# A router front of 28 hand-ordered steps: the transposes move one step behind the normalisation, logits and gates one step further

## The chip, the cores and the metric

The kernel runs on one core of a Trainium2 chip. The metric is the device time of one execution in microseconds (us). The core has a matrix engine (TensorE, PE in the rows), a vector engine (VectorE, DVE), a scalar engine (ScalarE, ACT), GpSimd (POOL) and SyncE (SP), which here only issues DMAs. Each engine works through its own list of instructions in order, and they wait for one another by semaphores.

## The reference

The program is one transformer-like stack over 16 sequences of 512 tokens of 256 features: attention, a mixture of experts, a forget attention, and the same mixture of experts again, each on a layer norm of its input and added to it. The part that matters is the mixture:

```
x      = layernorm(hidden)                      # 8192 x 256
logits = x @ router_w.T                         # 64 experts
probs  = softmax(logits); top 8 kept, rescaled to sum 1
routed = the 8 chosen experts' gated products (at most 128 slots a block), weighted
gu     = x @ ws_gate_up                         # shared expert
shared = (silu(gu[:, :192]) * gu[:, 192:]) @ ws_down
out    = hidden + routed + shared
```

## The kernel before

The program runs as blocks, one after another: `attention_project`, `attention_mix`, then `moe_front` and `moe_experts` for the first mixture (tiles named m1f and m1e), `forget_attention`, and `moe_front` and `moe_experts` again (m2f and m2e). The change is in `moe_front`, which therefore runs twice.

`moe_front` takes the 8192 tokens in 16 rounds of 512 (4 tiles of 128 tokens). For a round s it does this:

- SP loads x (`load`, L936, 512 KB) into a ring of 3.
- DVE takes mean and variance (`statistics` L1040, `aggregate` L1047) and POOL makes 1/deviation and shift (`inverse_deviation`, L997 to L1008).
- ACT normalises x into `row[:, s % 4]` (`normalise`, L1130, four instructions). `row` is a ring of RB = 4 buffers of 640 KB: 256 normalised features and 64 gates for each token.
- PE transposes the round in two halves (`turn_x(0)`, `turn_x(1)`, L1184) through one PSUM tile, `ps_x`, and ACT copies each half out (`keep(0)`, `keep(1)`, L1136). The second half waits until the first is copied out.
- PE computes the logits (L1193). DVE finds the eight largest (L1052), marks them, subtracts the largest, makes `chosen`; ACT takes the exponential (L1142); DVE picks and sums (`pick`, L1071 to L1075); POOL scales (`gates`, L1013), which fills the last part of the round's `row`.
- SP stores the finished `row` (`store_rows`, L944). Only when it has landed may `normalise` of round s + 4 write that buffer.
- PE counts tokens for each expert (`count_tiles`, L1200).
- The shared expert: `gate_up(0..2)` (L1212, twelve matmuls), silu on ACT (L1147, L1149), products on DVE (L1081, L1086), `down_first` and `down_rest` on PE (L1219, L1226), copies on ACT (`copy_down`, L1159), the residual (L940) added on POOL (L1020), and the store (L948).

All of it is ordered by hand. Each engine calls `in_turn(stages)` with a list of (at, stage, items). For s = 0 to STEPS - 1 = 27 it goes through the list and issues each stage whose `at(i)` is s. So an engine's order is: by step, and within the step by its list. There is no barrier between steps; an engine goes on as soon as its own waits allow.

Before the change round i is loaded and measured in step i, normalised and transposed in step i + 1, given logits in step i + 2, and gated, stored and counted in step i + 3. The shared expert's gate and up products of round r run in step 2r + 2 for r < 8 and in r + 10 after that, and the down product one step later. So up to step 17 two kinds of step alternate. In this text a G step has the gate and up products and a D step the down product. In steps 19 to 26 the places of the tokens are worked out for two groups of 4 experts a step (`climb` L1244 and L1245, `copy_rise` L1164 on ACT, `find_place` L1255, `count_below` L1103 on DVE), next to the last shared products. `count_reached` (L1262) ends it in step 27.

PE's list begins: `logits`, `turn_x(0)`, even `climb`, `gate_up(0)`, `down_first`, `turn_x(1)`, ... , `down_rest`, `gate_up(1)`, ..., `gate_up(2)`, `count_tiles`. ACT's list is `normalise`, `keep(0)`, `keep(1)`, `copy_rise`, `copy_down`, `exponential`, `silu`. SP's list is `load`, weight loads, `load_residual`, `store_rows`, `store`. The lines that the change's consequences hang on are these:

```
def normalise(s):
    act.wait_ge(shift_done, s + 1)
    wait(act, row_stored[s % RB], 16 * (s // RB))
...
def turn_x(q):
        pe.wait_ge(xn_done, TPR * s + 2 * q + 2)
        wait(pe, x_kept, 2 * s + q)
```

Of the kernel before, what the change touches and what calls it, by code (L numbers as in the profile page):

```python
# [10 lines left out]
def wait(eng, sem, value):  # L11

    if not isinstance(value, int) or value > 0:
        eng.wait_ge(sem, value)  # L14
# [784 lines left out]
def moe_front(nc, tag, dram, x_in, x_out, const):  # L799
# [8 lines left out]
    ROUNDS, S = TILES // TPR, TPR * P  # L808
# [5 lines left out]
    GROUPS = E // GROUP  # L814
    slots, slots_f = const["slots"], const["slots_f"]

    L_NORM, L_LOGITS, L_GATE = 1, 2, 3
    EARLY = ROUNDS // 2
    COUNTED = ROUNDS + L_GATE
    ASSIGN = [COUNTED + k // 2 for k in range(GROUPS)]  # L820

    def shared_at(r):
        return 2 * r + 2 if r < EARLY else r + EARLY + 2

    STEPS = shared_at(ROUNDS - 1) + 3

    with ExitStack() as ctx:
# [82 lines left out]
        def x_of(s):  # L910

            return const["ahead_x"][:].rearrange("p (t d) -> p t d", d=D) if ahead and s == 0 else x[:, s % XB]

        def kept_at(r):

            return (r - 6) % XT
# [4 lines left out]
        def in_turn(stages):  # L921

            for s in range(STEPS):
                for at, stage, items in stages:
                    for i in range(items):
                        if at(i) == s:
                            stage(i)

        @block.sync
        def _(sp):  # L930
# [41 lines left out]
            def load_kept(i):  # L972
                sp.wait_ge(gated, 3 * (last_round(i) + 1))
                load_weights(OWN + EARLY_BUFFERS + i)

            in_turn([(lambda i: i, lambda i: load(i + XB - 1), ROUNDS - XB + 1), (lambda i: ROUNDS + i, load_weights, OWN),
                     (lambda i: ROUNDS + L_GATE + 1 + i, load_early, EARLY_BUFFERS), (lambda i: shared_at(last_round(i)) + 1, load_kept, KEPT_BUFFERS),
                     (shared_at, load_residual, ROUNDS),
                     (lambda i: i + L_GATE, store_rows, ROUNDS), (lambda r: shared_at(r) + 1, store, ROUNDS)])
            sp.wait_ge(pad_stored, 16)  # L980
# [142 lines left out]
        @block.scalar  # L1123
        def _(act):
# [3 lines that stand above are left out]
                wait(act, x_was_turned, 2 * (s - RB + 1))  # L1128
                for t in range(TPR):
                    nc.scalar.activation(row[:, s % RB, t, 0:D], x_of(s)[:, t, :], ACT.Identity, bias=shift_x[:, s % 2, t], scale=rstd[:, s % 2, t]).then_inc(xn_done, 1)  # L1130

            def keep(q):
                def stage(s):
                    act.wait_ge(x_was_turned, 2 * s + q + 1)
                    wait(act, gated, 3 * (s - XT + 1))
                    nc.scalar.activation(x_turned[:, kept_at(s), :, 2 * q * P:2 * (q + 1) * P], ps_x[:], ACT.Copy).then_inc(x_kept, 1)  # L1136
                return stage

            def exponential(s):
                act.wait_ge(logit_done, s + 1)  # L1140
                wait(act, picked_done, s - 1)
                nc.scalar.activation(expd[:, s % 2], logit[:, s % 2], ACT.Exp).then_inc(exp_done, 1)  # L1142

            def silu(r):
                wait(act, h_done, 2 * (r - 1))
                act.wait_ge(gated, 3 * r + 1)
                nc.scalar.activation(act_g[:, r % 2, 0, :], ps_h[0][:], ACT.Silu).then_inc(silu_done, 1)  # L1147
                act.wait_ge(gated, 3 * r + 3)
                nc.scalar.activation(act_g[0:SR, r % 2, 1, :], ps_h[2][0:SR, :], ACT.Silu).then_inc(silu_done, 1)  # L1149

            def copy_down(r):
                wait(act, stored[r % 2], 16 * (r // 2))
                if r == 0 and ahead:

                    for landed, value in const["x_stored"]:
                        act.wait_ge(landed, value)
                act.wait_ge(down_done, r + 1)
                for q in range(2):
                    nc.scalar.activation(xo[:, r % 2, 2 * q:2 * q + 2, :], ps_d[q][:], ACT.Copy).then_inc(down_copied, 1)  # L1159

            def copy_rise(k):
                act.wait_ge(rise_ready, k + 1)
                wait(act, place_ready, k - 1)
                nc.scalar.activation(rise[:, k % 2], ps_x[0:E].rearrange("p c t -> p (c t)"), ACT.Copy).then_inc(rise_done, 1)  # L1164

            in_turn([(lambda i: i + L_NORM, normalise, ROUNDS), (lambda i: i + L_NORM, keep(0), ROUNDS), (lambda i: i + L_NORM, keep(1), ROUNDS), (lambda k: ASSIGN[k], copy_rise, GROUPS),
                     (lambda r: shared_at(r) + 1, copy_down, ROUNDS), (lambda i: i + L_LOGITS, exponential, ROUNDS), (shared_at, silu, ROUNDS)])

        @block.tensor
        def _(pe):  # L1170
# [7 lines left out]
            def turn_x(q):  # L1178
                def stage(s):
                    pe.wait_ge(xn_done, TPR * s + 2 * q + 2)  # L1180
                    wait(pe, x_kept, 2 * s + q)
                    for t in range(2):
                        for c in range(2):
                            last = nc.tensor.transpose(ps_x[:, c, t * P:(t + 1) * P], row[:, s % RB, 2 * q + t, c * P:(c + 1) * P], ident[:])  # L1184
                    last.then_inc(x_was_turned, 1)
                return stage
# [17 lines left out]
            def gate_up(i):  # L1204
                def stage(r):
                    if i == 0:
                        pe.wait_ge(x_kept, 2 * (r + 1))
                        wait(pe, silu_done, 2 * (r - 1) + 1)
                    else:
                        wait(pe, h_done, 2 * (r - 1) + i)  # L1210
                    for c in range(2):
                        last = nc.tensor.matmul(ps_h[i][:], w_gu[:, c, i, :], x_turned[:, kept_at(r), c, :], start=c == 0, stop=c == 1)  # L1212
                    last.then_inc(gated, 1)
                return stage
# [43 lines left out]
            def count_reached(k):  # L1258
                pe.wait_ge(rise_done, GROUPS)
                pe.wait_ge(reached_done, GROUPS)  # L1260
                for e in range(E):
# [3 lines left out]
            even = lambda k: ASSIGN[k] if k % 2 == 0 else -1  # L1265
            odd = lambda k: ASSIGN[k] if k % 2 else -1
            down_at = lambda r: shared_at(r) + 1
            in_turn([(lambda i: i + L_LOGITS, logits, ROUNDS), (lambda i: i + L_NORM, turn_x(0), ROUNDS), (even, climb, GROUPS),
                     (shared_at, gate_up(0), ROUNDS), (down_at, down_first, ROUNDS), (lambda i: i + L_NORM, turn_x(1), ROUNDS), (even, find_place, GROUPS),
                     (odd, climb, GROUPS), (down_at, down_rest, ROUNDS), (shared_at, gate_up(1), ROUNDS), (odd, find_place, GROUPS),  # L1270
                     (shared_at, gate_up(2), ROUNDS), (lambda i: i + L_GATE, count_tiles, ROUNDS), (lambda i: STEPS - 1, count_reached, 1)])

# [752 lines left out]
def program(nc, a):  # L2025
# [18 lines left out]
    def mixture(tag, x_in, x_out, x_stored):  # L2044
        with (nc.sbuf_tensor(tag + "_slots", [P, E], u32) as slots, nc.sbuf_tensor(tag + "_slots_f", [P, E], fp32) as slots_f,
              nc.sbuf_tensor(tag + "_own", [P, OWN * (GU + WD) - WD], fp32) as own, nc.sbuf_tensor(tag + "_early", [P, EARLY * (GU + WD)], fp32) as early,
              nc.sbuf_tensor(tag + "_kept", [P, KEPT * (GU + WD)], fp32) as kept):


            buffers = []  # L2050
            for memory, n in ((own, OWN), (early, EARLY), (kept, KEPT)):
                for k in range(n):
                    at = k * (GU + WD) - (WD if memory is own and k > 0 else 0)
                    down = ahead_x[0:F // 2, :] if memory is own and k == 0 else memory[0:F // 2, at + GU:at + GU + WD]
                    buffers.append((memory[:, at:at + GU].rearrange("p (j m c f) -> p j m c f", j=2, m=2, c=2),
                                    down.rearrange("p (j c d) -> p j c d", j=2, c=2)))
            const = dict(held, **landing, x_stored=x_stored, slots=slots, slots_f=slots_f, w_buffers=buffers, early=early, kept=kept, w_gate=a["L0_ffn_w_gate"], w_up=a["L0_ffn_w_up"], w_down=a["L0_ffn_w_down"])
            with nc.cleanup_on_exit():
                moe_front(nc, tag, routed, x_in, x_out, const)
            with nc.cleanup_on_exit():  # L2060
                moe_experts(nc, tag, routed, x_out, const)
# [69 lines left out]
```

## Time and profile before

| what | us |
|---|---|
| median of 3 runs (lowest, highest) | 2587.7 (2587.27, 2588.34) |
| the profiled execution, its time | 2572.92 |
| its span in the trace | 2571.3 |
| first front, from its first instruction to its last store | 1108.2 to 1348 |
| second front | 2090.4 to 2338 |
| granted TensorE clock, mean over the span | 0.961 |

The profiled execution is 14.8 us shorter than the median of the runs. In the rows, a time is in us from the start of the span; a line of the timeline gives start, duration, engine, source line, operation, tiles, the number of instructions merged, and in brackets how long the engine sat idle before it and what ended that. The granted clock is 1.00 at 2.4 GHz and 0.50 at 1.2 GHz.

### The profile page before, as it was taken

Reading aid. Unit: us, or ns where it says so; the run is one execution under the profiler, and the core shown is the slowest. Engines: PE = TensorE matmul, PEld = TensorE weight load, DVE = VectorE, ACT = ScalarE, POOL = GpSimd, SP = SyncE. Lnnn points to the kernel's source line nnn. Section 1 sums busy time; section 2 is a strip of 40 time slices with the busy share of each in tenths; the row PEclk is TensorE's granted clock in tenths of the full one; section 3 lists DMA queues with packets and bytes.
Section 4 is the critical chain, followed back from the end, with each engine's and each line's share of the span. In section 5 each row is a group of like instructions: output and inputs, shape, how many; then the busy total and the mean of one; then the engine's idle time right before and its main releaser. Section 6 shows DMA issues by size and latency. Waiting matters only on the chain. (4 is left out here: it accounts for less than half of the span.)

```text
span 2571.3 us, 47983 instructions
## 1 busy us (share of the span) xinstructions
PE 2413.5 (94%) x14630; PEld 1324.0 (51%) x14630; DVE 1650.9 (64%) x3745; ACT 1374.3 (53%) x2766; POOL 1151.7 (45%) x1497
## 2 busy tenths in 40 slices
PE   7997999999999999979999996999999969998998
PEld 4664233333333333356556774566666645655775
DVE  6777888888888888446553333788888746553332
ACT  4666677667766776646532333455555436632332
POOL 6998111110111011123226775777777723325776
PEclk9998799999999999989999998999999988898999
DMA  5655423232333332136777984011111025595996
GB/s 176 204 193 174 124 85 99 87 98 87 95 90 91 93 91 68 35 118 205 224 236 202 231 200 71 18 38 38 35 38 34 20 75 182 189 291 162 223 230 108
DMA packets 290964, 325.17 MB, mean 126 GB/s; under 512 B 30496, under 2 KB 272368, under 8 KB 290800
## 3 DMA queue, kind: packets, MB, share of 16 engines
q1 hardware_dynamic: 257024, 274.22, 35.3%
q0 software_dynamic: 29184, 46.43, 8.8%
q10 hardware_dynamic: 4592, 2.47, 0.4%
q8 instruction: 87, 1.43, 0.2%
q14 instruction: 77, 0.63, 0.1%
HBM read 217.29 MB, written 105.19 MB: 125 GB/s over the span
## 5 line engine op out<-in xcount | busy, mean ns | idle before, releaser
L716 DVE TENSOR_REDUCE a_row_max<-a_ps_m 128x2 f32<-128x1024 f32 x512 | 607.6, 1220 | 84.1 <-PE a_ps_m L619 79.3
L776 ACT ACTIVATE a_probs<-a_ps_s 128x512 f32<-128x512 f32 x1024 | 536.8, 601 | 206.4 <-PE a_ps_s L647 206.1
L662 PE MATMUL a_ps_o<-a_probs,a_va 128*32 128x512 f32 x2048 | 273.8, 607 | 0.8 <-ACT a_o_sb L785 0.8
L1731 POOL TENSOR_TENSOR b_spread<-b_decay,held_own_sb 128x512 f32<-128x512 f32 x256 | 269.2, 1084 | 8.2 <-DVE b_weight L1792 8.2
L1792 DVE TENSOR_TENSOR b_weight<-b_ps_s,b_spread 128x512 f32<-128x512 f32 x256 | 163.8, 683 | 17.6 <-PE b_ps_s L1932 17.6
L647 PE MATMUL a_ps_s<-first_qs,first_ks 98*128 98x512 bf16 (+1 forms) x512 | 160.8, 395 | 3.2 <-DMA first_qs<-a_m_parts 3.2
L647 PE MATMUL a_ps_s<-second 98*128 98x512 bf16 (+1 forms) x512 | 156.8, 386 | 4.8 <-DMA second<-a_m_parts 2.3
L556 POOL CAST a_high<-a_row_max 128x32 bf16<-128x32 f32 x32 | 6.6, 206 | 316.6 <-DVE a_row_max L716 316.6
L597 POOL DMA_DIRECT2D x<-a_xo x32 | 24.2, 757 | 274.0 <-DVE a_xo L750 271.6
L315 PE MATMUL a_ps_qk<-a_w_qk,a_xnT 128*128 128x512 f32 x256 | 121.7, 598 | 0.0
L619 PE MATMUL a_ps_m<-first_ks,first_qs 48*128 48x512 bf16 x512 | 106.4, 413 | 10.0 <-DVE a_row_max L716 9.3
L619 PEld LDWEIGHTS a_ps_m<-first_ks,first_qs 48*128 48x128 bf16 x512 | 24.7, 93 | 158.2 <-issue 90.5
L1212 PE MATMUL m2f_ps_h<-m_kept,held_ws_gate_up_sb 128*128 128x512 f32 x192 | 103.8, 677 | 0.0
L1868 ACT ACTIVATE b_o_sb<-b_ps_o,held_b_den_eps 128x512 f32<-128x512 f32 x64 | 44.0, 688 | 111.4 <-PE b_ps_o L1942 111.4
L619 PEld LDWEIGHTS a_ps_m<-second 48*128 48x128 bf16 x512 | 24.5, 92 | 147.7 <-issue 94.8
L1551 DVE SCALAR_TENSOR_TENSOR m1e_h<-m1e_act_g,m1e_xg,m1e_ps_h 128x192 f32<-128x192 f32 x64 | 26.5, 414 | 115.3 <-ACT m1e_act_g L1480 115.3
L1551 DVE SCALAR_TENSOR_TENSOR m2e_h<-m2e_act_g,m2e_xg,m2e_ps_h 128x192 f32<-128x192 f32 x64 | 26.5, 414 | 115.1 <-ACT m2e_act_g L1480 115.1
L619 PE MATMUL a_ps_m<-second 48*128 48x512 bf16 x512 | 99.8, 386 | 0.4
L1212 PE MATMUL m1f_ps_h<-m_kept,held_ws_gate_up_sb 128*128 128x512 f32 x192 | 100.0, 655 | 0.0
L198 POOL TENSOR_TENSOR a_qk<-a_rot_cos,a_rot_sin 128x512 f32<-128x512 f32 x64 | 81.4, 1272 | 7.5 <-DVE a_rot_sin L240 7.5
L647 PEld LDWEIGHTS a_ps_s<-second 98*128 98x128 bf16 (+1 forms) x512 | 37.8, 97 | 84.7 <-issue 39.6
L191 POOL TENSOR_TENSOR second<-a_rest,second 128x512 bf16<-128x512 f32 x64 | 74.2, 1160 | 10.9 <-ACT second L286 5.4
(397 smaller groups left out, 5454.2 us busy)
## 6 DMA issues: line engine op xcount, KB each, us to landing
parts<-second SPq DMA_DIRECT2D x16, 1536.0 KB, 6.2
second<-parts SPq DMA_DIRECT2D x384, 64.0 KB, 2.3
rows<-m_early SPq DMA_DIRECT2D x32, 640.0 KB, 3.2
m_early<-x SPq DMA_DIRECT2D x31, 512.0 KB, 4.0
first_qs<-parts SPq DMA_DIRECT2D x192, 64.0 KB, 2.3
first_ks<-parts SPq DMA_DIRECT2D x192, 64.0 KB, 2.2
m_own<-in_L_ffn_w_gate_dram SPq DMA_DIRECT2D x24, 384.0 KB, 4.3
m_own<-in_L_ffn_w_up_dram SPq DMA_DIRECT2D x24, 384.0 KB, 5.6
```

Source lines behind the costliest of these rows:

```text
L191: nc.gpsimd.tensor_tensor(parts[:, k // TPB, 2, :, j * P:(j + 1) * P], rest[:, u, :].rearrange("p (g t) -> p g t", g=4), parts[:, k // TPB ...
L198: nc.gpsimd.tensor_tensor(qk[:, u, :], rot_cos[:, u, :], rot_sin[:, u, :], ALU.add).then_inc(qk_done, 1)
L315: last = nc.tensor.matmul(ps_qk[u][:], xnT[:, u, c, :], w_qk[:, c, :], start=c == 0, stop=c == 1)
L619: last = nc.tensor.matmul(m_bank(name, step)[:, e, :], qs[u][rows, 2 * n.p + e, t * P:(t + 1) * P], ks[u][rows, 2 * n.p + e, :], start=Tru ...
L647: nc.tensor.matmul(s_bank(name, step)[:], ks[u][0:K_ALL[e], h, t * P:(t + 1) * P], qs[u][0:K_ALL[e], h, :], start=True, stop=True).then_in ...
L662: last = nc.tensor.matmul(ps_o[VW * j:VW * (j + 1), :], va[n.u][:, t, (h0 + j) * VW:(h0 + j + 1) * VW], probs[:, group % 2, j, t, :], star ...
L716: nc.vector.tensor_reduce(row_max[:, n.k // 4 % 2, t, :, n.p % 4], m_bank(name, step)[:], AX.X, ALU.max).then_inc(m_drained, 1)
L776: nc.scalar.activation(probs[:, group % 2, j, t, :], s_bank(name, step)[:], ACT.Exp, scale=DK ** -0.5).then_inc(s_drained, 1)
L1212: last = nc.tensor.matmul(ps_h[i][:], w_gu[:, c, i, :], x_turned[:, kept_at(r), c, :], start=c == 0, stop=c == 1)
L1551: nc.vector.scalar_tensor_tensor(h[:, i % 2, j, :], act_g[:, i % 2, j, :], xg[:, i % XB, j, D + e:D + e + 1], ps_h[j][:, 1, :], ALU.mult, ...
L1731: nc.gpsimd.tensor_tensor(spread[:, n % 2, heads].rearrange("p h t c -> p (h t) c"), decay[:, n % 3, heads].rearrange("p h (t o) -> p (h t ...
L1792: nc.vector.tensor_tensor(weight[:, n % 2, heads, :], ps_s[r][:].rearrange("p h (j t) -> p (h j) t", t=P), spread[:, n % 2, heads].rearran ...
```

## The change

Round i is still measured in step i and normalised in step i + 1. It is transposed in step i + 2 (new constant L_TURN), given logits in step i + 3, and gated, stored and counted in step i + 4. The shared products of rounds 0 to 7 move from step 2r + 2 to 2r + 3; those of rounds 8 to 15 stay in r + 10. COUNTED and with it the steps of the places become 20 to 27 instead of 19 to 26. The number of steps (28), the order within each list, and all ring sizes stay. No instruction is added or removed.

```diff
-    L_NORM, L_LOGITS, L_GATE = 1, 2, 3
+    L_NORM, L_TURN, L_LOGITS, L_GATE = 1, 2, 3, 4
     EARLY = ROUNDS // 2
     COUNTED = ROUNDS + L_GATE
     ASSIGN = [COUNTED + k // 2 for k in range(GROUPS)]
 
     def shared_at(r):
-        return 2 * r + 2 if r < EARLY else r + EARLY + 2
+        return 2 * r + 3 if r < EARLY else r + EARLY + 2
...
-            in_turn([(lambda i: i + L_NORM, normalise, ROUNDS), (lambda i: i + L_NORM, keep(0), ROUNDS), (lambda i: i + L_NORM, keep(1), ROUNDS), (lambda k: ASSIGN[k], copy_rise, GROUPS),
+            in_turn([(lambda i: i + L_NORM, normalise, ROUNDS), (lambda i: i + L_TURN, keep(0), ROUNDS), (lambda i: i + L_TURN, keep(1), ROUNDS), (lambda k: ASSIGN[k], copy_rise, GROUPS),
...
-            in_turn([(lambda i: i + L_LOGITS, logits, ROUNDS), (lambda i: i + L_NORM, turn_x(0), ROUNDS), (even, climb, GROUPS),
-                     (shared_at, gate_up(0), ROUNDS), (down_at, down_first, ROUNDS), (lambda i: i + L_NORM, turn_x(1), ROUNDS), (even, find_place, GROUPS),
+            in_turn([(lambda i: i + L_LOGITS, logits, ROUNDS), (lambda i: i + L_TURN, turn_x(0), ROUNDS), (even, climb, GROUPS),
+                     (shared_at, gate_up(0), ROUNDS), (down_at, down_first, ROUNDS), (lambda i: i + L_TURN, turn_x(1), ROUNDS), (even, find_place, GROUPS),
```

## Rows read from the trace of the kernel before

**Rows 1.** The page: busy time of each engine and share of the span.
```profile
PE 2413.5 (94%) x14630; PEld 1324.0 (51%) x14630; DVE 1650.9 (64%) x3745; ACT 1374.3 (53%) x2766; POOL 1151.7 (45%) x1497
```

**Rows 2.** Waits of TensorE, first front, steps 4 to 16: total, times, longest.
```profile
PE m1f_ps_x L1184 <- ACT m_early L1130: 10.2, 7, 1.5
```

**Rows 3.** Stretches: length; busy PE, PEld, DVE, ACT, POOL; granted clock, DMA share, GB/s.
```profile
1139.70:1246.40 106.70, 97.98 (x504) 64.86 (x504) 67.53 (x319) 71.07 (x122) 41.19 (x73) 0.92 0.56 182
2123.60:2236.40 112.80, 104.03 (x504) 67.78 (x504) 67.65 (x320) 71.33 (x122) 41.30 (x73) 0.86 0.54 173
1208.90:1214.20 5.30, 5.30 (x13) 3.13 (x14) 3.65 (x13) 1.48 (x3) 3.17 (x6) 0.50 0.84 270
```

**Rows 4.** Timeline of TensorE: a D step, a G step, next logits; the last pair.
```profile
1148.21 2.00 PE L1193 MATMUL m1f_ps_l<-m1f_rwT,m_kept 128*128 128x64 f32 x16
...
1152.51 0.66 PE L1184 MATMUL m1f_ps_x<-held_ident_sb,m_early 128*128 128x128 f32 x4
...
1154.51 2.00 PE L1193 MATMUL m1f_ps_l<-m1f_rwT,m_kept 128*128 128x64 f32 x16
1157.92 0.66 PE L1184 MATMUL m1f_ps_x<-held_ident_sb,m_early 128*128 128x128 f32 x4 [1.41 <-ACT m_early L1130]
1160.13 0.60 PE L1184 MATMUL m1f_ps_x<-held_ident_sb,m_early 128*128 128x128 f32 x4
1160.57 3.60 PE L1212 MATMUL m1f_ps_h<-m_kept,held_ws_gate_up_sb 128*128 128x512 f32 x8
...
1164.65 2.00 PE L1193 MATMUL m1f_ps_l<-m1f_rwT,m_kept 128*128 128x64 f32 x16
...
1246.51 1.12 PE L1184 MATMUL m1f_ps_x<-held_ident_sb,m_early 128*128 128x128 f32 x4 [1.47 <-ACT m_early L1130]
...
1256.16 2.00 PE L1193 MATMUL m1f_ps_l<-m1f_rwT,m_kept 128*128 128x64 f32 x16
```

**Rows 5.** Timeline of ScalarE, the same D and G steps.
```profile
1154.07 1.09 ACT L1159 ACTIVATE m1f_xo<-m1f_ps_d 128x512 f32<-128x512 f32 x2 [0.27 <-PE m1f_ps_d L1219]
1155.17 1.28 ACT L1142 ACT_TABLE_LOAD   x1
1156.46 0.42 ACT L1142 ACTIVATE m_early<-m_early 128x256 f32<-128x256 f32 x1
1156.79 2.06 ACT L1130 ACTIVATE m_early<-m_early,m1f_shift_x,m1f_rstd 128x256 f32<-128x256 f32 x4
1158.76 0.58 ACT L1136 ACTIVATE m_kept<-m1f_ps_x 128x512 f32<-128x512 f32 x1
...
1164.69 2.06 ACT L1130 ACTIVATE m_early<-m_early,m1f_shift_x,m1f_rstd 128x256 f32<-128x256 f32 x4
```

**Rows 6.** Timeline of SyncE's DMA issues, the same G step.
```profile
1156.53 0.37 SPq L944 DMA_DIRECT2D rows<-m_early  x1
1159.39 0.51 SPq L936 DMA_DIRECT2D m_early<-x  x1
1159.94 1.05 SPq L940 DMA_DIRECT2D m1f_xr<-x  x1
1163.34 0.37 SPq L944 DMA_DIRECT2D rows<-m_early  x1
```

**Rows 7.** The row stores (L944) by themselves: in that D step, then all of them.
```profile
DMA to landing us min/median/max: 3.2/3.2/3.2
...
DMA to landing us min/median/max: 3.2/3.2/8.4
```

**Rows 8.** Timeline, filling of the first front.
```profile
1115.56 0.20 POOL L1008 TENSOR_TENSOR m1f_shift_x<-m1f_minus_mean,m1f_rstd 128x4 f32<-128x4 f32 x1
...
1116.47 1.09 PE L1184 MATMUL m1f_ps_x<-held_ident_sb,m_early 128*128 128x128 f32 x4 [0.78 <-ACT m_kept L1136]
```

**Rows 9.** Timeline of TensorE and ScalarE, the last step with places.
```profile
1342.58 0.38 PE L1255 MATMUL m1f_ps_l<-m1f_rise,m1f_reached 64*128 64x128 bf16 x4
...
1343.57 0.59 ACT L1164 ACTIVATE m1f_rise<-m1f_ps_x 64x512 bf16<-64x512 f32 x1 [3.40 <-PE m1f_ps_x L1245]
```

## The prediction

> **What bounds the kernel now.** I read the page first, then the waits of TensorE, then busy times by stretch, and last the timeline of three engines over one pair of steps. TensorE is busy 94% of the span [rows 1] and the blocks follow one another, so a front that is longer by 1 us makes the program longer by 1 us. A measurement tells a change from none from about 0.2% on (5.2 us). Inside the first front TensorE waits seven times for the normalisation, 10.2 us in all [rows 2]; the second front shows the same seven. Each stands where a G step follows a D step. The timeline shows why: ScalarE has copy_down, a table load and the exponential to do (1154.07 to 1156.88) before it starts `normalise` at 1156.79 [rows 5], and the transposition wants its first two tiles, so it starts at 1157.92 after 1.41 us of idle [rows 4].
>
> The clock costs as much again. A pair of steps takes 1164.65 - 1148.21 = 16.44 us where the clock stays at 2.4 GHz [rows 4]. Six pairs of the first front take 106.7 us and six of the second 112.8 us [rows 3], 17.78 and 18.80 us a pair, so 1.34 and 2.36 us a pair, 1.85 on average, go to a lower clock. After one of those waits the granted clock is 0.50, that is 1.2 GHz, for 5.3 us [rows 3]. The last G step takes 1256.16 - 1246.51 = 9.65 us from its first transpose instead of 1164.65 - 1157.92 = 6.73 us [rows 4], 2.92 us more.
>
> **What moves.** No instruction is added, so busy time at full clock is unchanged. TensorE's order up to the last transposition is the old one, one step number later. Relative to it, only ScalarE's `normalise`, the statistics on VectorE and GpSimd and SyncE's `load` run one step earlier. So I lay the new steps over the times of the pair in rows 4 to 6.
>
> *What is removed.* `turn_x(0)` uses rows normalised a step ago. It starts 1.41 us earlier, and left alone `turn_x(1)` would start at 1160.13 - 1.41 = 1158.7.
>
> *What is late next.* `normalise(s)` writes `row[s % 4]` and waits for the store of round s - 4 to land. Before, that store was issued in step s - 1, and `normalise(s)` is in step s + 1: a whole step of slack. Now `gates`, and `store_rows` behind it, are one step later, so the store is issued in step s, just ahead of the normalisation that waits for it. In the D step the store is issued at 1156.53 [rows 6] and takes 3.2 us to land [rows 7]. It hangs on the logits of the D step through VectorE and GpSimd, none of which moves against TensorE. It lands at 1159.73. `normalise`, ready at 1156.79 as before [rows 5], is held 2.95 us.
>
> Queued behind it on ScalarE is `keep(0)`, and `turn_x(1)` needs that copy. So: landing 1159.75, four normalisations of 2.06 us to 1161.8, the copy 0.6 us to 1162.4, some 0.14 us to TensorE (an estimate: half of the normalisations of 1156.79 are over at 1157.8, and the transposition that wants them starts at 1157.92 [rows 4, 5]), `turn_x(1)` at 1162.55. It was at 1160.13 [rows 4]: **+2.4 us a pair**. TensorE idles from about 1158.8, some 3.8 us in one piece instead of 1.4.
>
> The landing may differ. The store is alone in the queues at this point of the pair, as it was before, so 3.2 us is the value; the largest landing of a row store is 8.4 us [rows 7], for stores behind weight loads, which do not exist in these steps.
>
> The Trainium skill (DMA: Bandwidth & Descriptors, section Anatomy of one DMA) gives a DMA about 2.0 us of fixed cost and then its bytes at 436 GB/s. For 640 KB that is an estimate of 3.5 us where this trace has 3.2, which would add 0.3 us to each of twelve waits and give 2624.5. Its fixed part also says that a smaller store would still be held up, which no run here shows.
>
> *How often.* `normalise(4)` is the first with an earlier user of its buffer. It and rounds 6, 8, 10, 12 and 14 fall where a G step follows a D step: six a front, twelve in all.
>
> *The clock in these twelve pairs.* It was 1.85 us a pair. The new gap is longer, and the row nearest to a sure drop is the last pair, 2.92. I take 2.2, between them. The bounds are 0 (as in the pair of rows 4, which waited and lost nothing) and everything behind the gap at half speed, `turn_x(1)` and eight matmuls, 0.5 + 3.6 us [rows 4], so +4.1. Each pair then changes by 2.4 + 2.2 - 1.85 = 2.75 us, **12 x 2.75 = +33.0**; with the bounds 2.4 + 0 - 1.85 = 0.55 and 2.4 + 4.1 - 1.85 = 4.65.
>
> *The last pair of each front.* There is no round 16, so nothing is held and `turn_x(0)` doesn't wait: 1.47 and 2.92 us are saved [rows 4]. **2 x -4.4 = -8.8.**
>
> *Filling.* `normalise(1)` now comes ahead of `keep(0)` of round 0. Its shift is ready at 1115.76 [rows 8]; 2.06 and 0.6 us later, with 0.14, `turn_x(1)` of round 0 starts at 1118.55, not 1116.47 [rows 8]. **2 x 2.1 = +4.2.** The first waits of `normalise(0)` are the same.
>
> *Step 18.* It now has the logits of round 15, and `silu` of round 8 stands behind copy_down, the exponential and two table loads: 1.09 + 1.28 + 0.42 + 1.28 + 0.6 = 4.7 us [rows 5] (the last two are the same kinds of instruction), 5.0 with its start. TensorE has four to five microseconds of products behind `down_rest` to cover it. I take 0.5; bounds 0 and 1. **+1.0.**
>
> *The tail.* Steps 19 to 25 of before hide two groups' places behind shared products; now one such pair of groups runs in step 27 with nothing beside it. A find and a climb take TensorE from 1342.58 to about 0.1 us before ScalarE copies the climb's result at 1343.57 [rows 9], 0.88 us. Bare, each of two groups costs 0.88 and the copy between them, 0.59 [rows 9] with two handovers of 0.1 to 0.2, about 1.65; with the end of copy_down ahead of the first (0.3) it is 3.6. 1.76 of it is taken out of a covered step. 3.6 - 1.76 = 1.85, **2 x = +3.7**; bounds 2 and 5.
>
> *Queues.* `store_rows` passes the next `load` on SyncE, and `gates` the next `inverse_deviation` on GpSimd. Neither waits longer than the store did: the load goes out when the held `normalise` ends (1161.8), before the gates of the G step are ready (about 1163.3 [rows 6]). SyncE's residual load then takes until 1163.45. Stage weight loads of steps 16 to 19 now share the queues with one more row store; nobody waits for that one, so 0.
>
> Sum: 33.0 - 8.8 + 4.2 + 1.0 + 3.7 = **+33.1 us**. On the profiled execution 2572.9 + 33.1 = 2606.0. Its time is 14.8 us below the median of the runs, and I put the same sum on the median: 2587.7 + 33.1 = **2620.8**, 1.3% slower. Without the twelve pairs the other terms give 0.1.
>
> **Rivals.**
>
> *A: the row has landed in time.* This is the other side. `normalise` then starts at 1156.79, ends at 1158.85, `keep(0)` at 1159.4, `turn_x(1)` at 1159.55: 0.6 us better a pair, and a gap of 0.85 us may keep the clock up, 0 to 1.85 more. 12 x (0.6 to 2.45) gives 7 to 29 us faster, 2558 to 2581, middle 2570. For it: no row before shows a wait for a row store. Against it: the store would have to be issued 2.95 us earlier, and it ends a chain that doesn't move. Without clock effects the balance tips where the landing comes before 1157.4.
>
> *B: the clock pays.* One long idle is no dearer than a short one and no clock is lost in the twelve pairs. 12 x 0.55 + 0.1 = +7, 2594; with a part of the clock loss, or of C, up to 2612.
>
> *C: the wait in the D step as well.* The G step's row store is issued at about 1163.5, right behind a load and a residual load of 512 KB each, which before had 3.9 and 3.4 us of lead [rows 6]. `normalise` of the D step is ready with the D step's logits (1164.69 beside 1164.65 [rows 4, 5]), and TensorE feels it only 1.5 us later, since `turn_x(1)` comes 1152.51 - 1148.21 = 4.3 us after the logits start [rows 4] and normalising and copying take 2.8. With 2.2 us of clock loss TensorE feels it from 1170.75. At 8.4 us the store lands at 1171.9: up to +1.1 a pair, 2634. With the full clock loss of 4.1 us this wait is covered, and the sum is +56, 2644. C stands for this upper side.
>
> *D: a wash.* The clock gives back what the wait takes, pair by pair, within 0.4 us; 2583 to 2593.
>
> **How the numbers follow.** Forecast, 2.0 to 3.6 us a pair, 2612 to 2631: 0.58. B, 2594 to 2612: 0.14. C, above 2631: 0.15. A: 0.08. D: 0.05. Leaving out A, D, the lower part of B and the end of C gives 2600 to 2640 for 8 in 10. Slower by over 0.2%: 0.58 + 0.14 + 0.15 = 0.87; within: 0.05; faster: 0.08.
>
> **What the changed profile would show.** `normalise` (L1130) on ScalarE idle for about 3 us until a DMA of `rows`, six times a front, and TensorE's waits on L1184 then put down to the copy L1136, 3 to 4 us each, instead of 1.4 for L1130. Pairs of 20 to 22 us in steps 5 to 16 with a granted clock of 0.75 to 0.85, then a pair of about 15 us at 1.00. The second transpose of round 0 about 2 us later. Two finds at the end with idle between. If ScalarE doesn't idle ahead of L1130, my step on the ring is wrong; if it does and TensorE's pairs are no longer than 18 us, the clock term is.

## The result, and the profile after

| | before | after |
|---|---|---|
| median of the runs | 2587.48 | 2617.61 |
| lowest and highest of 4 runs each | 2583.42 to 2588.34 | 2614.50 to 2619.55 |
| ratio, 95% interval | | 1.0103 [1.0078, 1.0128] |
| profiled execution, its span | 2571.3 | 2615.9 |

The changed kernel is 30.1 us slower (the median of before is of four runs here, of three in the table ahead of the prediction). Forecast was 2620.8. The busy time of the page answers to [rows 1]: PE is where it was (2413.5 us), and only its share of a longer span falls.

```profile
PE 2413.7 (92%) x14630; PEld 1321.5 (51%) x14630; DVE 1646.8 (63%) x3745; ACT 1373.2 (52%) x2766; POOL 1150.1 (44%) x1497
```

The waits of TensorE in steps 5 to 16 of the first front, beside [rows 2]: there are six now, not seven, they have moved from the normalisation (L1130) to the copy (L1136), and one lasts 3.9 us in the mean instead of 1.5.

```profile
PE m1f_ps_x L1184 <- ACT m_kept L1136: 23.5, 6, 4.4
```

Busy times by stretch, columns as in [rows 3]: six pairs of the first front, six of the second, the part of one pair behind its wait, and one whole pair.

```profile
1137.16:1261.78 124.62, 101.09 (x505) 65.14 (x505) 66.44 (x312) 71.32 (x121) 41.45 (x71) 0.90 0.50 162
2150.30:2274.71 124.41, 101.47 (x505) 64.20 (x504) 65.95 (x312) 71.36 (x121) 41.44 (x71) 0.90 0.50 162
1187.63:1193.87 6.24, 6.24 (x17) 2.92 (x17) 0.69 (x1) 3.23 (x5) 0.76 (x2) 0.73 0.86 272
...
1193.87:1214.40 20.53, 16.70 (x85) 10.80 (x84) 11.24 (x53) 11.85 (x21) 6.88 (x12) 0.92 0.51 166
```

Twelve pairs take 249.0 us; they took 219.5 [rows 3]. The timeline of TensorE through one G step, then the last pair of the front, beside [rows 4]:

```profile
1181.93 1.88 PE L1212 MATMUL m1f_ps_h<-m_kept,held_ws_gate_up_sb 128*128 128x512 f32 x4
1187.63 0.85 PE L1184 MATMUL m1f_ps_x<-held_ident_sb,m_early 128*128 128x128 f32 x4 [3.81 <-ACT m_kept L1136]
1188.28 5.11 PE L1212 MATMUL m1f_ps_h<-m_kept,held_ws_gate_up_sb 128*128 128x512 f32 x8
...
1261.78 2.00 PE L1193 MATMUL m1f_ps_l<-m1f_rwT,m_kept 128*128 128x64 f32 x16
...
1270.30 2.00 PE L1193 MATMUL m1f_ps_l<-m1f_rwT,m_kept 128*128 128x64 f32 x16
```

The eight matmuls behind the wait take 5.11 us where the same eight took 3.60 [rows 4]. ScalarE in the same G step and the row store ahead of it on SyncE, beside [rows 5] and [rows 6]:

```profile
1181.66 0.42 ACT L1142 ACTIVATE m_early<-m_early 128x256 f32<-128x256 f32 x1
1184.93 2.08 ACT L1130 ACTIVATE m_early<-m_early,m1f_shift_x,m1f_rstd 128x256 f32<-128x256 f32 x4 [2.85 <-issue]
1186.92 0.57 ACT L1136 ACTIVATE m_kept<-m1f_ps_x 128x512 f32<-128x512 f32 x1
```

```profile
1181.66 0.37 SPq L944 DMA_DIRECT2D rows<-m_early  x1
```

The store is issued at 1181.66, and the normalisation starts 3.27 us later, which is the 3.2 us of a landing [rows 7] and a handover. The waiting instruction is put down to "issue" here, not to the DMA. Only the same wait in the D steps carries the DMA's name. All of ScalarE's waits at L1130 in these steps:

```profile
ACT m_early L1130 <- issue: 17.8, 6, 3.5
ACT m_early L1130 <- DMA rows<-m_early: 3.7, 5, 1.4
```

The copy at 1186.92 is queued behind the normalisation, though its input has lain ready since the transposition of 1181.49, and `turn_x(1)` at 1187.63 waits for that copy.

At the ends of the front, beside [rows 8] and [rows 9]: the second transposition of round 0, and the two finds of the last step with their waits.

```profile
1118.18 1.09 PE L1184 MATMUL m1f_ps_x<-held_ident_sb,m_early 128*128 128x128 f32 x4 [2.84 <-ACT m_kept L1136]
...
1359.39 0.40 PE L1255 MATMUL m1f_ps_l<-m1f_rise,m1f_reached 64*128 64x128 bf16 x4 [0.82 <-ACT m1f_rise L1164]
...
1361.03 0.39 PE L1255 MATMUL m1f_ps_c<-m1f_rise,m1f_reached 64*128 64x128 bf16 x4 [0.68 <-ACT m1f_rise L1164]
```

### The profile page after: what moved, and what is told of

The parts are those of the page before. It is cut to its first block and busy times, and to the rows that moved or that the text cites. A ratio compares the mean times of both kernels' runs of the same rounds, so it can differ in the third digit from the quotient of the medians.

```text
span 2615.9 us, 47983 instructions
## 1 busy us (share of the span) xinstructions
PE 2413.7 (92%) x14630; PEld 1321.5 (51%) x14630; DVE 1646.8 (63%) x3745; ACT 1373.2 (52%) x2766; POOL 1150.1 (44%) x1497
```

## The theory and its rivals

**Theory.** Moving the transposition is no loss in itself. `row` has four buffers, and the change puts the gates and the store of round s - 4 into step s, right ahead of the step s + 1 in which round s is normalised. The whole step of slack between them is gone, so ScalarE stands 2.9 us at `normalise`, and `keep(0)`, next on its list, holds up TensorE. The gap then costs clock as well. **Rival 1:** the order of ScalarE's list is the cause by itself, store or no store. **Rival 2:** the loss lies in the filling and the longer tail. **Rival 3:** the loss lies in the expert blocks, which no line of the diff touches but which are longer in the trace after.

The last rival has something in the profile for it. The two fronts, from the first L1172 to the first L1262, are 28.5 us longer in sum than in the profile before. The spans differ by 44.6. Another 17 us are in the expert blocks, from the first to the last L1403: 203.3 and 200.6 us instead of 193.5 and 193.4.

## The experiments

All ratios are to runs of the kernel before beside it. The median of those runs was not always the same: 2587.5 us for the first row, 2586.3 for the last two, 2578.2 for "after, 5 row buffers", "before, 3 row buffers", "after, keep(0) ahead of normalise" and "after, four matmuls issued twice", and 2592.3 for the rest. So it is ratios that are compared, and where an expectation is in us, the ratio times 2587.5 is what answers it. "Fronts" is the length of the two fronts in sum, less the 480.9 us of before; it is from one profile of each kernel.

| run | ratio [95%] | fronts |
|---|---|---|
| after | 1.0103 [1.0078, 1.0128] | +28.5 |
| after, again | 1.0097 [1.0069, 1.0125] | +21.4 |
| after, 5 row buffers | 0.9904 [0.9884, 0.9924] | -30.5 |
| before, 3 row buffers | 1.0178 [1.0148, 1.0207] | +44.4 |
| before, 5 row buffers | 0.9982 [0.9965, 0.9999] | -6.2 |
| after, keep(0) ahead of normalise | 0.9952 [0.9935, 0.9969] | -11.5 |
| after, four matmuls issued twice | 1.0043 [1.0026, 1.0060] | +5.4 |
| after, 5 buffers and keep(0) first | 0.9825 [0.9801, 0.9849] | -46.0 |
| after, L_GATE = 3 | 0.9892 [0.9867, 0.9918] | -33.8 |
| after, L_GATE = 3 and keep(0) first | 0.9824 [0.9796, 0.9853] | -49.6 |
| before, again | 1.0001 [0.9978, 1.0024] | -0.2 |

**A fifth row buffer.** The changed kernel with RB = 5. To make room, the ring of x moves into `own`, a region that is free in these steps. The last weight load of the front, which also lands there, waits until the last round is normalised, and the count of stores that a later load wants follows the new ring. (The lines that hand `own` to the front and make the weight load wait are left out of the cut below.)

```diff
-    XB, RB = 3, 4
+    XB, RB = 3, 5
...
-        x = in_early("k t d", [XB, TPR, D])
+        x = const["own"][:, 4096:4096 + XB * TPR * D].rearrange("p (k t d) -> p k t d", k=XB, t=TPR)
...
-                        sp.wait_ge(row_stored[k], 16 * ROUNDS // RB)
+                        sp.wait_ge(row_stored[k], 16 * len(range(k, ROUNDS, RB)))
```

> The changed kernel with five row buffers instead of four (x moved to other memory to make room), nothing else. Theory (the ring: normalise waits for a row store issued just before it): the store now has a whole step more, ScalarE's wait of 2.9 us ahead of L1130 goes away in all twelve pairs, and TensorE waits at most some 0.8 us for keep(0) behind normalise. The pairs fall from 20.6 us to 16 to 18, the total to 2557 to 2579, faster than before. Rival (ScalarE's order alone, keep behind normalise and the exponential, makes the wait): nothing changes, 2617, TensorE still waits 3.8 us.

Measured: 2552.63 us, 0.9904, which on 2587.5 is 2562.7 and in the range of the theory. ScalarE has no wait at L1132 (L1130 of after) in these steps any more, and TensorE's six waits of 3.9 us are down to 0.86 each. A pair takes 15.87 us at a granted clock of 1.00, just under the 16 to 18 expected. The waits of TensorE in steps 5 to 16, and one pair by stretch:

```profile
PE m1f_ps_x L1186 <- ACT m_kept L1138: 5.1, 6, 0.9
```

```profile
1185.68:1201.55 15.87, 15.01 (x85) 9.99 (x84) 11.25 (x54) 11.77 (x21) 6.88 (x13) 1.00 0.71 217
```

This change takes the whole loss away and uncovers a gain of 1%. Of rival 1 only 0.86 us a pair is left, and rival 2 falls: the filling and the tail are as in the changed kernel (from the first L1172 to the G step from which the pairs are counted 29.0 and 32.2 us instead of 29.3 and 32.0, and from the last logits to the first L1262 91.0 us in both), and this one is faster than before.

**The same loss put into the kernel before.** RB = 3, with the order of before. The count of stores follows the ring here too.

```diff
-    XB, RB = 3, 4
+    XB, RB = 3, 3
...
-                        sp.wait_ge(row_stored[k], 16 * ROUNDS // RB)
+                        sp.wait_ge(row_stored[k], 16 * len(range(k, ROUNDS, RB)))
```

> The kernel before with three row buffers instead of four, nothing else. It puts before's normalise in the same relation to the row store as the change does, with the old steps. Theory (the ring): normalise is held to the landing in seven G steps a front; turn_x(0) starts about 3.0 us later, and with the clock's share each of 14 pairs grows by 3 to 4 us: 2630 to 2645. Rival (the slowdown needs the moved transposes): no effect, 2587.

Measured: 2620.57 us, 1.0178, which on 2587.5 is 2633.6, as expected. With three buffers the kernel before has the distance that the changed one has with four, and it gets the same wait on ScalarE. TensorE's and ScalarE's waits from 1138 to 1256 us, which hold six of the seven G steps; TensorE waits 4.45 us in the seventh:

```profile
PE m1f_ps_x L1184 <- ACT m_early L1130: 26.4, 6, 4.4
```

```profile
ACT m_early L1130 <- issue: 17.0, 6, 2.9
ACT m_early L1130 <- DMA rows<-m_early: 1.0, 2, 0.6
```

**A control.** RB = 5 in the kernel before, with all the edits of the first experiment.

> The kernel before with five row buffers (x moved to the same other memory), nothing else: the control for the moved memory and the longer ring. Theory (before has a whole step of slack on four buffers): no effect, ratio 0.998 to 1.002, still seven waits of 1.4 us a front. Rival (the moved x or the longer ring is itself what gains with five buffers): 0.990.

Measured: 2586.32 us, 0.9982 [0.9965, 0.9999], with the seven waits of [rows 2] as they were, 10.2 us. A fifth buffer alone brings 0.2%, and by the interval 0.35% at most; the 2% between the changed kernel with four and with five buffers is the wait and the clock behind it. (The 6.2 us that its fronts are shorter in the table are all in the second front, where TensorE's waits are the 1.4 to 1.5 us of before and the clock fell less behind them.)

**ScalarE's order.** The changed kernel with four buffers, `keep(0)` ahead of `normalise`, `keep(1)` behind it.

```diff
-            in_turn([(lambda i: i + L_NORM, normalise, ROUNDS), (lambda i: i + L_TURN, keep(0), ROUNDS), (lambda i: i + L_TURN, keep(1), ROUNDS), ...
+            in_turn([(lambda i: i + L_TURN, keep(0), ROUNDS), (lambda i: i + L_NORM, normalise, ROUNDS), (lambda i: i + L_TURN, keep(1), ROUNDS), ...
```

> The changed kernel with four row buffers, but in ScalarE's list keep(0) stands ahead of normalise, and keep(1) behind it. normalise is still held by the row store. Theory (what costs time is that keep(0) is queued behind the held normalise): TensorE's 3.8 us before turn_x(1) fall below 1 us though ScalarE still waits about 2 us for the row; pairs of 15 to 16 us, total 2547 to 2560. Rival (the row wait itself bounds the pair whatever stands behind it): 2617, the wait moves to turn_x(0) of the next step.

Measured: 2565.73 us, 0.9952, which on 2587.5 is 2575.1. The direction was right, and the time missed the expected 2547 to 2560 by at least 15 us. I had taken the held normalisation to be harmless once `keep(0)` was out of its way. But `keep(1)` is behind it still, and the logits of the next step read what `keep(1)` writes. The wait moved there. TensorE's and ScalarE's waits in these steps:

```profile
PE m1f_ps_l L1193 <- ACT m_kept L1136: 9.2, 5, 3.4
PE m1f_ps_d L1219 <- DVE m1f_hT_rest L1086: 3.1, 5, 0.9
```

```profile
ACT m_early L1130 <- DMA rows<-m_early: 19.4, 6, 5.0
ACT m_early L1130 <- issue: 7.6, 4, 2.0
```

ScalarE stands still for 27.0 us, more than the 21.5 of after, and the kernel is faster all the same. It is what is queued behind a wait that counts, not how long the wait is.

**Work in the gap.** The changed kernel, with the first four matmuls of `gate_up` (1.88 us) issued twice in rounds 1 to 6. They write the same result again and stand just ahead of the wait.

```diff
-                    for c in range(2):
-                        last = nc.tensor.matmul(ps_h[i][:], w_gu[:, c, i, :], x_turned[:, kept_at(r), c, :], start=c == 0, stop=c == 1)
+                    for again in range(2 if i == 0 and 1 <= r <= 6 else 1):
+                        for c in range(2):
+                            last = nc.tensor.matmul(ps_h[i][:], w_gu[:, c, i, :], x_turned[:, kept_at(r), c, :], start=c == 0, stop=c == 1)
```

> The changed kernel, with the four matmuls of gate_up(0) issued twice for rounds 1 to 6 (the second time over the first, same values). That is 12 x 1.9 us of extra work for TensorE, placed in the 3.8 us in which it idles. Theory (the clock drop behind the gap is part of the price, 1.7 us a pair): the extra work costs nothing, the gap is 1.9 us, and 0 to 20 us come back: 2597 to 2617, the more pairs keep 2.4 GHz the less. Rival (TensorE is the bound there, or the clock drop doesn't hang on the gap's length): 2617 to 2640.

Measured: 2589.75 us, 1.0043, which on 2587.5 is 2598.6 and in the range of the theory, near its lower end. The changed kernel measures 1.0103 and 1.0097, so this one is 14 to 16 us faster with 22.6 us of matmuls more. The granted clock stays at 1.00 and the pair takes 18.84 us, not 20.53:

```profile
1191.00:1209.84 18.84, 16.77 (x90) 10.75 (x89) 11.01 (x53) 11.86 (x21) 6.88 (x12) 1.00 0.56 176
```

So 1.7 us of this pair of the changed kernel is the clock and not the wait. The six pairs of each front take 113.1 us here, both times at a clock of 1.00; that is 18.85 us a pair, against 20.75 in the mean of the changed kernel's twelve, and 1.9 us is the clock's part.

**The changed kernel once more.**

> The changed kernel again, beside the others on one chip. The ratio of 1.010 comes again. The two expert blocks, whose length differed by 17 us between the two first traces, tell whether that difference belongs to the change: if it does, they take 203 and 201 us again; if it is spread from run to run, anything from 193 to 203.

Measured: 2614.69 us, 1.0097. Its first front has pairs of both kinds, with no edit:

```profile
1150.07:1168.93 18.86, 15.05 (x85) 9.99 (x85) 10.80 (x53) 11.87 (x21) 6.88 (x12) 1.00 0.56 186
1228.52:1248.96 20.44, 16.60 (x85) 10.84 (x85) 11.30 (x53) 11.85 (x21) 6.88 (x12) 0.92 0.48 154
```

That confirms the two parts of the price: 18.86 with the wait alone, 1.6 more where the clock falls. It is also why the first front of this profile is 7 us shorter than that of the first profile (246.2 and 253.4 us). The expert blocks take 201.8 and 200.8 us, close to the 203.3 and 200.6 of the first profile; what that says is settled below, by the kernel before.

**The store one step earlier.** The changed kernel with four buffers and L_GATE back at 3. The gates, the row store and the count run in the same step as the logits, where the changed kernel has them one step behind, and the places are worked out in steps 19 to 26 again.

```diff
-    L_NORM, L_TURN, L_LOGITS, L_GATE = 1, 2, 3, 4
+    L_NORM, L_TURN, L_LOGITS, L_GATE = 1, 2, 3, 3
```

> The changed kernel with L_GATE 3 instead of 4: gates, row store and count stay in the step of the logits, one step less than in the change; four row buffers, ScalarE's order as changed. Theory (the ring): the store goes out a step earlier, normalise is never held, pairs of about 15.9 us as with five buffers, and the tail of places is not exposed (5 us): ratio 0.985 to 0.992. Rival (VectorE, now waiting in the same step for the exponential, delays the next largest-of-eight and the logits): 0.995 to 1.005, with TensorE waiting on VectorE.

Measured: 2562.27 us, 0.9892, as expected. The slack is back by time instead of by memory. ScalarE doesn't wait at L1130, TensorE waits as with five buffers:

```profile
PE m1f_ps_x L1184 <- ACT m_kept L1136: 5.1, 6, 0.9
```

**Both holds removed.** Five buffers with `keep(0)` first, and then L_GATE = 3 with `keep(0)` first, each a sum of edits shown above.

> Five row buffers and ScalarE's order keep(0), normalise, keep(1), together. Theory (two separate waits, the row store and keep(0) behind normalise): the 0.86 us that TensorE still waits before turn_x(1) with five buffers goes too, and the filling is 1.5 us shorter a front: 12 x 0.86 + 3 = 13 us below the version with five buffers alone, a ratio of about 0.985 to before, pairs of 15.0 us. Rival (keep(1) behind normalise then holds copy_down and the logits of a D step): no better than 0.990.

> The changed kernel with four row buffers, L_GATE = 3 (gate_up and the row store one step earlier) and ScalarE's order keep(0), normalise, keep(1). Theory (two separate holds on ScalarE: the store of the same step, and normalise queued ahead of keep): with the store a step early and keep(0) first neither is left, so this should run like the version with the fifth buffer and keep(0) first: ratio to before 0.979 to 0.986 (about 2540 to 2552 us), a pair of steps about 14.8 us, no wait of m_ps_x over 1 us, and no wait of the logits on keep(1). Rival (the store one step earlier is released by gate_up's own step, so normalise is still held in some steps and now holds keep(1)): ratio 0.988 to 0.996, waits of the logits on keep(1) of 1 to 3 us. Rival 2 (only L_GATE = 3 counts, keep's place costs nothing any more): 0.989, as L_GATE = 3 alone.

(Where the second says `gate_up`, it is the `gates` that move with L_GATE.) Measured: 2546.47 us, 0.9825, and 2541.55 us, 0.9824. The two ways are equal within their intervals, and the first came out a little better than the 0.985 expected. With `keep(0)` first the last 0.86 us of a pair goes too. In the second of them TensorE has no wait in steps 5 to 16, and the only one from 1138 to 1250 us is this, behind the last logits. A pair takes 14.83 us:

```profile
PE m1f_ps_h L1212 <- ACT m1f_act_g L1147: 0.5, 1, 0.5
```

```profile
1147.04:1161.87 14.83, 14.83 (x86) 10.08 (x85) 10.92 (x54) 11.73 (x21) 7.12 (x13) 1.00 0.73 233
```

This version beats both kernels, by 1.8% the one before and by 2.8% (0.9824 / 1.0103) the changed one, and needs no memory more.

**The kernel before once more,** for the third rival.

> The kernel before once more, as a second profile of it. Ratio 1.000 within 0.002. Theory (the expert blocks vary by several us from run to run with the granted clock, the fronts hardly): first to last L1403 of each layer anywhere from 193 to 204 us, and the fronts' length, first L1172 to first L1262, within 3 us of 236.6 and 244.3 us. Rival (the change made the expert blocks longer): 193 to 195 us again in both layers.

Measured: 2588.83 us, 1.0001. The instructions that bound the expert blocks, in this profile of the kernel before; the last two columns of times are the first and the last start:

```profile
L1403 PE MATMUL m1e_ps_r<-held_ident_sb,m_slots_f x64: 273/275/579, 1351.9 to 1553.6; 128*128 128x128 f32 x64
L1403 PE MATMUL m2e_ps_r<-held_ident_sb,m_slots_f x64: 273/275/582, 2352.0 to 2551.1; 128*128 128x128 f32 x64
```

201.7 and 199.1 us, where the first profile of the same kernel had 193.5 and 193.4. Its fronts are the same within 0.2 us. Over all twelve profiles an expert block takes 193 to 207 us, whichever the kernel. The fairest pair is the kernel before with five buffers and the changed kernel once more, which ran on one chip: 199.4 and 201.1 beside 201.8 and 200.8 us, 2.1 us in sum. Rival 3 falls: of the 17 us this pair leaves 2.1 to the change, less than two profiles of one kernel differ by, and the fronts, 28.5 us longer, account for nearly all of the 30.1. The first profile of before had expert blocks 13.9 us shorter in sum than the second, which would account for most of the 14.8 us by which it lay below the median.

## Why the prediction was right

The direction, the place and most of the sizes were as forecast, and in one place two misses cancel. The terms, against the two profiles:

| term | forecast | measured |
|---|---|---|
| twelve held pairs | +33.0 | +29.6 |
| last pair of each front | -8.8 | -9.1 |
| filling | +4.2 | +3.3 |
| step 18 and tail | +4.7 | +4.7 |
| sum | +33.1 | +28.5 |

The measured column is worked out from the starts of the logits of G steps (249.03 less 219.46; twice 8.5 instead of 13.1), from the first L1172 to the first of those, and from the last of them to the first L1262. The medians differ by 30.1.

- **The hold on ScalarE.** Forecast 2.95 us behind a store that lands after 3.2, six times a front; measured 2.83 to 3.48, six times, 17.8 us. Three experiments show it as the cause, two by taking it away, with a buffer and with a step, and one by putting it in. The Trainium skill (DMA: Bandwidth & Descriptors, section Anatomy of one DMA) has 2.0 us and the bytes at 436 GB/s as its fit for DMAs on the GpSimd path, an estimate of 3.5 us for this size. This store is issued by SyncE. From its issue to the start of the normalisation it is 3.27 us here, handover included, so the row of before was the better term.
- **What the wait costs without the clock.** 16.44 + 2.4 = 18.84 us a pair was forecast; pairs of 18.84 and 18.86 us at a clock of 1.00 were measured. In the second the wait falls in two pieces, 1.59 us in the D step and 2.21 in the G step. TensorE's gap was forecast as 3.8 us and is 3.81 to 3.85 in ten of the twelve pairs, 4.39 and 3.07 in the others.
- **The clock.** This is the term that was mis-sized. I took 2.2 us a pair, between the 1.85 of before and the 2.92 of one pair. Measured is 249.0 / 12 - 18.84 = 1.9. Twelve times 0.3 is the 3.5 us by which the main term is off. There was no row of before for a gap of this length, and in the mean the longer gap cost hardly more clock than the 1.85 of before. The granted clock of the pairs was forecast as 0.75 to 0.85 and is 0.90. That was a slip even by the forecast's own sum: 2.2 us lost are 4.4 us at half speed, and in a pair of 21 us that makes 0.90. The pair behind them takes 14.82 us at 1.00, as forecast.
- **Last pair, filling, tail.** Nothing is held in the last pair, as forecast. In the filling `turn_x(1)` of round 0, counted from the first L1172, came 2.05 us later in the first front, as forecast, and 1.4 in the second. In the tail the two finds wait 0.8 and 0.7 us. Behind the last logits TensorE waits 1.0 us for `silu` where 0.5 was taken; twice 0.5 more there leaves 2.8 us for the tail in place of the 3.7 forecast, so that row of the table agrees because two misses cancel.
- **Rival A** (the row lands in time) is what the kernel does with a fifth buffer or an earlier store. Its price was right too: a wait of 0.85 us and 7 to 29 us in all were worked out for it. The two variants have a wait of 0.86 us and no clock loss, and are 25 and 28 us faster than before (0.96% and 1.08% of 2587.5), its upper end.
- **Rival B** (the clock pays): with matmuls in the gap, where it does pay, the kernel is at 1.0043. By itself the clock stayed up in only three of the twenty-four held G steps of the two profiles of after.
- **Rival C** (a wait in the D step too) is there: five waits of 0.3 to 1.4 us, 3.7 in all. Where the clock has fallen TensorE feels none of them in the first front and one in the second, 0.73 us at 2252.95, with 3.07 instead of 3.83 at the next G step. Where the clock stays up it feels one too: 1.59 us, with 2.21 at the next G step. The prediction added such a wait to the pair, but both times the pair as a whole is no longer for it, 20.55 and 18.86 us, since the next wait is shorter by as much. So the upper side that C stands for did not come.
- **Rival D** (a wash) is out: each of the twelve pairs is 2.5 us longer in the mean.
- **The shift to the median.** The profile's own time lay 14.8 us below the median, and I put the sum on the median. That was right, as the second profile of before shows; the difference of the two spans, 44.6 us, would have misled by 14.5. That rests on two profiles of before.

What the prediction didn't see is how cheap the mending is: the gates and the store needn't have moved with the logits.

## What to carry to other kernels

When a stage is moved back in a hand-ordered pipeline, count for each ring the steps between the last use of a buffer and its next writing, with the DMA's landing in it. One step too few here turned a gain of 1.0 to 1.1% into a loss of 1.0%, and either one more buffer or one stage left where it was would have kept it. On an engine that works through its list in order, put what others wait for ahead of what may itself be held: that alone brought the changed kernel from 1.0103 to 0.9952, and together with the slack it gives 1.8%. Where one profile's blocks differ though nothing in them changed, profile the old kernel a second time before explaining it.

## What the runs showed of the hardware

- **Useless work can pay.** Twelve times 1.88 us of repeated matmuls, put ahead of a gap of 3.8 us, made the kernel 14 to 16 us faster, and the granted clock stayed at 1.00 in all twelve pairs.
- **The same wait doesn't always cost the clock.** In the same G step of the first front both profiles of the changed kernel show an idle of 3.83 us. In one of them four transpositions and eight matmuls behind it take 1.09 and 5.75 us, in the other 0.63 and 3.60. So the price given here is a mean over many pairs.
- **The length of the gap alone doesn't decide.** The kernel before waits 1.41 to 1.49 us in each of its fourteen G steps, and in twelve of them the step then takes 11.6 us or more instead of the 10.1 to 10.2 of the other two. With the repeated matmuls there are waits of up to 2.12 us, and none is followed by a lower clock. The runs don't show what does decide, the length of the gap together with the work before it or something else.
- **Blocks that weren't touched vary.** An expert block took 193 to 207 us over twelve profiles. The two fronts in sum agreed within 0.2 us in the two profiles of the kernel before and differed by 7 in the two of the changed kernel. Here the difference of spans between two single profiles, 44.6 us beside 30.1 for the medians, said less than the sum of the terms that one can point to.
